# A decoder layer with post-norm attention and experts: the two halves of each block of exponentials' scores issued apart on TensorE

## What is computed

```python
q = x @ w_q.T; k = x @ w_k.T; v = x @ w_v.T          # split into 16 heads of 16
scores = jnp.einsum('bqhd,bkhd->bhqk', q, k) * scale
weights = jax.nn.softmax(scores, axis=-1)
out = jnp.einsum('bhqk,bkhd->bqhd', weights, v)
x = _layernorm(x + concat(out) @ w_o.T)
```

## Time and profile before

| | us |
|---|---|
| median of 3 runs | 1513.89 |
| lowest and highest | 1512.09, 1513.94 |
| the profiled execution, whole | 1512.49 |
| its span in the profile | 1510.7 |
| TensorE busy | 1426.7 |
| VectorE busy | 968.2 |
| ScalarE busy | 823.6 |

### The profile page before, as it was taken

How to read it: one execution, slowest core, us unless ns; L and a number is a source line. 1 busy time by engine, 2 the same in 40 slices (tenths; PEclk the granted TensorE clock), 3 DMA queues, 4 the chain that set the end, 5 groups by cost and what they waited for, 6 DMA issues and landing times.

```text
span 1510.7 us, 47820 instructions
## 1 busy us (share of the span) xinstructions
PE 1426.7 (94%) x18566; PEld 903.6 (60%) x18566; DVE 968.2 (64%) x1679; ACT 823.6 (55%) x1966; POOL 388.4 (26%) x677
## 2 busy tenths in 40 slices
PE   7999999999999999999999897999999999999990
PEld 3344444444444444444444346889999999999980
DVE  6777788888888888888888953555433323233226
ACT  3476777777777767777767682333333333333330
POOL 1211121212222225321225211354522222222223
PEclk9799999999999999999999999999999999999995
DMA  4224222433344223322343225233422222222226
GB/s 158 91 67 151 62 86 85 125 114 118 115 119 131 84 77 120 95 77 71 101 117 106 71 65 166 50 82 78 95 56 37 36 37 39 41 37 36 36 26 226
DMA packets 112255, 131.55 MB, mean 87 GB/s; under 512 B 26049, under 2 KB 89809, under 8 KB 111905
## 3 DMA queue, kind: packets, MB, share of 16 engines
q1 hardware_dynamic: 93760, 101.68, 22.7%
q0 software_dynamic: 14000, 19.48, 7.2%
q10 hardware_dynamic: 4272, 7.34, 1.4%
HBM read 76.51 MB, written 51.94 MB: 85 GB/s over the span
## 4 chain that ended last, share of the span: by engine, by line
PE 82%; DVE 8%; issue 3%; ACT 2%; DMA 2%; SPq 1%; DVEq 0%; POOL 0%; POOLq 0%; ACTq 0%
PE pa L1067 16%; PE pb L1078 15%; PE pb L852 14%; PE pa L852 14%; PE po L1022 12%; PE px L852 6%; DVE neg L1339 4%; PE px L845 2%; ACT w_sb L1151 2%; PE po L948 1%; PE px L923 1%; PE px L898 1%; DVE w_sb L1780 1%; DMA x<-space,y_tag 0%; SPq L451 0%
## 5 line engine op out<-in xcount | busy, mean ns | idle before, releaser
L1339 DVE TENSOR_REDUCE neg<-pa 128x1 f32<-128x1024 f32 x512 | 613.7, 1216 | 116.6 <-PE pa L852 96.0
L1151 ACT ACTIVATE w_sb<-pb 128x512 f32<-128x512 f32 x996 | 540.8, 596 | 174.8 <-PE pb L852 172.0
L852 PE MATMUL pb<-w_sb 99*32 99x512 bf16 x3984 | 325.3, 384 | 9.4 <-ACT w_sb L1151 6.5
L1264 ACT ACTIVATE space<-pa,b1T_sb 128x128 f32<-128x128 f32 x568 | 154.4, 383 | 329.6 <-PE pa L1067 329.6
L852 PE MATMUL pa<-w_sb 96*32 96x512 bf16 (+1 forms) x4208 | 318.9, 386 | 13.0 <-DVE neg L1339 11.9
L1067 PE MATMUL pa<-xgT,attn_t 128*128 128x128 f32 x2272 | 271.2, 277 | 8.3 <-DVE attn_t L1683 8.3
L1067 PEld LDWEIGHTS pa<-xgT,attn_t 128*128 128x128 f32 x2272 | 268.7, 193 | 12.3 <-issue 8.8
L1022 PE MATMUL po<-w_sb,space 128*32 128x256 f32 x4096 | 266.2, 378 | 1.3 <-ACT w_sb L1151 1.1
L1078 PE MATMUL pb<-w_sb,space 128*128 x1136 | 260.1, 379 | 0.0
L852 PEld LDWEIGHTS pb<-w_sb 99*32 99x32 bf16 x3984 | 104.5, 95 | 202.6 <-ACT w_sb L1151 126.6
L1078 PEld LDWEIGHTS pb<-w_sb,space 128*128 128x128 f32 x1136 | 208.9, 190 | 24.8
(11 more groups left out here) (209 smaller groups left out, 982.0 us busy)
## 6 DMA issues: line engine op xcount, KB each, us to landing
xg<-x_by_expert SPq DMA_DIRECT2D x71, 130.0 KB, 2.5
attention_out<-space SPq DMA_DIRECT2D x64, 128.0 KB, 1.8
w_sb<-w SPq DMA_DIRECT2D x16, 512.0 KB, 5.0
q_parts<-w_sb SPq DMA_DIRECT2D x48, 128.0 KB
w_sb<-q_parts SPq DMA_DIRECT2D x64, 96.0 KB, 2.5
w_sb<-k_parts SPq DMA_DIRECT2D x64, 96.0 KB, 2.6
k_parts<-w_sb SPq DMA_DIRECT2D x45, 128.0 KB
w_sb<-w SPq DMA_DIRECT2D x5, 1024.0 KB, 8.5
```

Of the source, the lines that this page charges most:

```text
L852: mm = pe.matmul(out[at:end], lhsT[:, at:end], rhs, start=start, stop=stop, tile_position=(0, at))
L1151: act.activation(ex[:, n % 4, half * HALF:(half + 1) * HALF], score_bank(n, half), ACT.Exp, scale=SCALE).then_inc(e_done, 1)
L1264: ins = act.activation(hT[tile % 2][:, f, :], pH[tile % 2][:, f, :], ACT.Relu, bias=g.b1_sb[:, bass.ds(e * FT + f, 1)])
L1339: dve.tensor_reduce(neg[i % 2][:, t:t + 1], pa[n % 2][:, :], AX.X, ALU.max, negate=True).then_inc(max_done, 1)
```

## The change

Only TensorE's list is touched; the lists of the four other engines, DMA issues included, are row for row the same. `score_exp` takes the half as an argument, `sums` takes one block in place of a pair, and the main loop puts one unit between any two halves: the sums of block 2p - 2, the sums of block 2p - 1, and max A. The wait of each half is unchanged. The sums of a block now wait for the exponentials of that block alone.

```diff
-                def score_exp(n):
+                def score_exp(n, half):
+                    i, t = divmod(n, TB)
+                    if t == 0 and half == 0:
+                        pe.wait_ge(rows_in[i % RING], 16 * (i // RING + 1))
+                    if in_pa(n):
+                        pe.wait_ge(max_done, NH * TB - 1 + n % 2)
+                        pe.wait_ge(e_done, 2 * n - 3 + half)
+                    elif n:
+                        pe.wait_ge(e_done, 2 * n - 1 + half)
+                    quarters(score_bank(n, half), ks[i % RING][:, t * P:(t + 1) * P],
+                             qs[i % RING][:, half * HALF:(half + 1) * HALF], True, True).then_inc(b_done, 1)
...
-                    pe.wait_ge(e_done, 4 * p + 4)
-                    for n in (2 * p, 2 * p + 1):
-                        t = n % TB
...
+                    pe.wait_ge(e_done, 2 * n + 2)
+                    for j in range(4):
...
+                    if n % 2:
+                        mm.then_inc(pv_done, 1)
...
                 for p in range(PAIRS):
-                    score_exp(2 * p)
+                    score_exp(2 * p, 0)
                     if p:
-                        sums(p - 1)
-                    score_exp(2 * p + 1)
+                        sums(2 * p - 2)
+                    score_exp(2 * p, 1)
+                    if p:
+                        sums(2 * p - 1)
+                    score_exp(2 * p + 1, 0)
                     if p + LEAD < PAIRS:
                         score_max(2 * (p + LEAD))
+                    score_exp(2 * p + 1, 1)
                     side(p)
                     if p + LEAD < PAIRS:
                         score_max(2 * (p + LEAD) + 1)
-                sums(PAIRS - 1)
+                sums(2 * PAIRS - 2)
+                sums(2 * PAIRS - 1)
```

More of the change, by code:

```diff
@@ L997, in score_max, with sums @@
                     mm.then_inc(a_done, 1)
-                def score_exp(n):
+                def score_exp(n, half):
[9 more added lines that the diff above has]
+                             qs[i % RING][:, half * HALF:(half + 1) * HALF], True, True).then_inc(b_done, 1)
+                def sums(n):
                     i, t = divmod(n, TB)
                     if t == 0:
[L1002 to L1014, removed]
                         pe.wait_ge(v_ready, i + 1)
@@ L1017, in sums @@
                             pe.wait_ge(o_out, i)
-                    pe.wait_ge(e_done, 4 * p + 4)
-                    for n in (2 * p, 2 * p + 1):
-                        t = n % TB
[L1021 to L1025, removed]
+                    pe.wait_ge(e_done, 2 * n + 2)
+                    for j in range(4):
+                        mm = pe.matmul(po[32 * j:32 * j + VW, 0:QC], vs[i % 2][:, t, :],
+                                       ex[:, n % 4, j * QC:(j + 1) * QC], start=t == 0, stop=t == TB - 1,
+                                       tile_position=(0, 32 * j))
+                    if n % 2:
+                        mm.then_inc(pv_done, 1)
                 pe.wait_ge(w_in, 32)
```

## The result

The changed kernel takes 1487.08 us (median of 4 runs, 1485.73 to 1490.55), the kernel before 1512.99 (4 runs, 1511.58 to 1513.94) in the same comparison. The ratio is 0.9833, 95% interval 0.9814 to 0.9852: 26 us faster. The forecast was 1483.5, its range 1476 to 1494.

The account below looks back on a forecast made before the run. TensorE's sets and its waits for ScalarE were taken to bound the loop. Gains of 18.1 + 11.0 + 1.0 = 30.1 us off 1512.5 gave 1482.4, with 1.4 for the median 1483.8, stated as 1483.5; range 1476 to 1494.

Parts of the forecast that it names:

- Ordinary pairs: Loop pairs without the s = 6 delay: 2.67 us falls to 2.59, a gain of 226 x 0.08 = 18.1 us.
- the 0.08 goes to zero and no new wait takes its place: The second block's scores lose 0.08 us a pair waiting for ScalarE; evenly spaced halves each have 0.21 to spare.
- Changes of kind: TensorE switching between sets of pb, po and so on, three to four more a pair: costed at nothing, bounds 0 and 0.11.
- The rival "drain": Each new change of kind on TensorE costs time: gain gone at 0.035 us each, 1580 at 0.11; chance 0.05 with other losses.
- The loop: The loop over pairs 0 to 247, 832.2 us before: shorter by 29 us.
- s = 5 into s = 6: Second block's scores at s = 6, late through the cross attention's exponential: 0.24 us lost for 0.74, gain 22 x 0.50 = 11.0.
- The rival that it takes ScalarE's place: Pairs with much VectorE work all wait at max B: 15 us less gain, 1498; chance 0.10.
- Pairs that VectorE holds and that lose their gain: Few pairs inside longer VectorE runs, near the ends of batches, lose their 0.08: about 0.8 us for ten.
- Taking nothing for the late turns: An earlier max B at s = 0 gains 0.8 us, set equal to the 0.8 lost in VectorE's longer runs.
- Last 8 pairs: ScalarE bounds them; some five idle gaps of 0.22 us shrink: gain 1.0 us, bounds 0 to 1.5.
- Behind the loop: The expert tiles after the loop: shifted one for one by the loop's end, their stretch unchanged.

Follow-up runs that it names:

- first_apart: Kernel before the change with only block 2p's halves pulled apart, the second block's left together: 1543.98 us, ratio 1.0199.
- second_apart: Kernel before the change with only the second block's halves pulled apart, block 2p's left together: 1493.29 us, ratio 0.9863.
- rows_96: Changed kernel with the exponentials' scores made from 96 rows in place of 99, minus maxima left out, a quarter of the scale: 1485.49 us, ratio 0.9812.
- Two independent edits: On the changed kernel, max A ahead of the second block's sums (p mod 4 not 0; ratio 0.9769), or the cross attention's exponential moved into s = 6 (0.9805).
- halved maxima: VectorE's maxima taken over 512 of 1024 columns, on the changed kernel (1495.65 us, ratio 0.9718) and on the kernel before (1511.63 us, 0.9836).
- after_again: The changed kernel itself, unaltered, measured again beside the kernel before: 1486.5 us, ratio 0.9816.
- max_first: Changed kernel with max A right behind the pair's first half, before both blocks of sums (p mod 4 not 0): ratio 0.9892.
- soft_later: Changed kernel with the cross attention's exponential moved from behind s = 5's four exponentials to between the blocks of s = 6: 1507.6 us, ratio 0.9805.

## Why the prediction was right, and where it was 4 us off

**Ordinary pairs.** The step "the 0.08 goes to zero and no new wait takes its place" holds: the second block's half 1 no longer waits, and each half stands 0.65 behind the last. The same chart gave the turn of first_apart (25.3 expected, 25.30 measured) and nearly the pair of second_apart (0.22 of wait expected, 0.23 measured). The size was off: the pair fell by 0.066 and not 0.08, to 2.607 and not 2.59.

**Changes of kind.** This is the term that was mis-sized. The prediction cost them at nothing, because starts in a timeline rounded to 0.01 us show no 0.004. In the trace after, a set that is the first of its kind takes 0.218 to 0.220 up to the next set's start and a second one 0.215, and a pair has eight firsts where it had four. Four more at 3.5 ns are 0.014 a pair, which is the difference between 0.080 and 0.066. At the 2 to 2.5 ns that the pairs' lengths of rows_96 and second_apart give, they are 0.008 to 0.010, and some 0.005 of the difference stay open; the 0.08 itself was a difference of starts rounded to 0.01. The rival "drain" named the mechanism's place, but at a thirtieth of the price at which it was stated (0.11) and a tenth of the one at which it decides (0.035). That the shortfall is this cost is argued from the starts and supported by the two kernels with fewer changes; it was not isolated.

**The loop.** Forecast 29.1 shorter, measured 25.7, so 3.4 less. 248 pairs at 0.014 would be 3.5, but that this comes out so evenly is luck: profiled again, the changed kernel's loop was 27.5 shorter, 1.6 less than forecast. By groups of turns the forecast has 5.8, 15.9 and 7.4 for turns 0 to 8, 9 to 23 and 24 to 30; the first execution gives 3.8, 14.0 and 7.9, the second 3.4, 14.1 and 10.0. The middle group, which is the same in both, is short by 1.9 and 1.8, near what the changes of kind cost at 0.014 a pair (15 x 8 x 0.014 = 1.7). In the first group there is also the pair at s = 1 that VectorE holds. The late turns gain more than was forecast.

**s = 5 into s = 6.** Forecast 0.24 late, measured 0.22; the second half waits for nothing, as said. Of the 0.93 that a turn with all side jobs gains, seven ordinary pairs give 7 x 0.066, and 0.47 are left for this place, where 0.50 were forecast. Two independent edits took this wait away, so the chain is shown.

**VectorE.** The rival that it takes ScalarE's place fell: its waits in the loop went from 59 to 48. The ordinary pairs are as long with halved maxima. Pairs that VectorE holds and that lose their gain, as the prediction allowed, are there: the one at s = 1 in the turns of p = 40 to 71. Taking nothing for the late turns was too little; they fell by 1.13, 0.2 more than the turns before them.

**Last 8 pairs.** Forecast 1.0, measured 1.5.

**Behind the loop.** Not in the sum, which took this stretch as unchanged: 2.0 us. The chain that ended last has, between the loop and the expert tiles, the last head's output going to memory and back. Before:

```profile
909.55 4.34 DMA attention_out<-space
914.35 6.02 DMA o_sums<-attention_out
922.23 6.40 PE pa L1067 x32
```

After:

```profile
881.89 6.06 DMA attention_out<-space
888.41 5.76 DMA o_sums<-attention_out
896.03 5.51 PE pa L1071 x32
```

The store took 6.06 in place of 4.34 us. All the profiles have 604.2 to 605.9 us behind the last exponential and only the one of before 603.3; even the slower first_apart has 605.8, and the changed kernel itself had 604.3 the second time. So it varies by 1 to 2 us from one execution to the next and is not shown to be the change's.

Together 25.7 + 1.5 - 2.0 = 25.2 us in the spans, and 25.9 in the medians, for 30.1 forecast; beside after_again the medians are 28.0 apart. So the 3.6 us between forecast and time are partly the term for changes of kind and partly one execution's difference from another.

## What to carry to other kernels

Where one engine fills two banks in turn and another empties them, try the fills at even distances that are at least the emptying time plus the signal: here 0.65 us for an exponential of 0.60. Pulling only one of two pairs of fills apart moves the delay into the other and can cost more than it takes. Before moving a unit ahead, read which buffer it waits for, because a unit that waits at the head of an in-order list holds up everything behind it (max_first).

## What was not expected of the hardware

Up to the next set's start, a set of four column strips takes 0.215 us behind one of its own kind and 0.218 to 0.220 as the first of a new one, though all are 32 columns wide; with one form in place of two for the scores the pair lost 7 ns (rows_96). A step into the transpose costs 0.10 to 0.11 over a set, before the change and after. On the second chip the kernel before took 1.6% longer (1538.4 against 1513.0 to 1514.5). In the four kernels profiled there the excess lies in the four turns in which GpSimd scatters rows, and in the one that was looked at (soft_later, 555 to 560 us) TensorE's sets start in pieces; the cause was not looked for.
